# Spacing the indirect DMAs of an attention kernel with routed experts: scatters at eight places over four steps, and the tail's sends deferred over twelve buffers

## What is computed

```python
h = layernorm(x) * (1 + ca) + sa
x = x + ga * attention(h)       # 16 heads of 8, causal softmax, layernorm, output projection
h = layernorm(x) * (1 + cb) + sb
x = x + gb * experts(h)         # 8 experts; each token goes to the best 2 by bid
# experts: sum over the 2 chosen of w_e * (silu(h @ gate_e.T) * (h @ up_e.T)) @ down_e.T
```

## Time and profile before

| | |
|---|---|
| median of 3 runs | 632.87 us (631.29 to 634.27) |
| the profiled execution | 636.49 us; its span from first to last instruction 634.7 us |
| mean granted TensorE clock | 0.945 of full |
| busy share of the span | TensorE 89%, VectorE 74%, ScalarE 64%, GpSimd 38% |
| indirect DMAs | 64 scatters, 71 sends, about 1 us of GpSimd each |

### The profile page before, as it was taken

How to read it: one execution, slowest core, us unless ns; L and a number is a source line. 1 busy time by engine, 2 the same in 40 slices (tenths; PEclk the granted TensorE clock), 3 DMA queues, 4 the chain that set the end, 5 groups by cost and what they waited for, 6 DMA issues and landing times.

```text
span 634.7 us, 16553 instructions
## 1 busy us (share of the span) xinstructions
PE 565.4 (89%) x5257; PEld 424.8 (67%) x5258; DVE 471.2 (74%) x1592; ACT 405.9 (64%) x716; POOL 244.1 (38%) x328
## 2 busy tenths in 40 slices
PE   5778999999898998998998987999888999999940
PEld 3455565666465565564564546999887999999930
DVE  5898787899797787796896863687765666667636
ACT  4425787878777786786786775686534655655612
POOL 5401301133723615416326243456554333343326
PEclk9597999999999898998998996999989999999975
DMA  4442668432333232322323011111321211111138
GB/s 125 132 121 70 176 173 224 130 110 74 95 93 93 82 93 72 103 77 71 106 82 93 3 36 27 40 44 53 103 78 53 53 50 50 42 50 50 40 124 289
DMA packets 61511, 56.82 MB, mean 90 GB/s; under 512 B 11156, under 2 KB 55572, under 8 KB 61444
## 3 DMA queue, kind: packets, MB, share of 16 engines
q1 hardware_dynamic: 56548, 44.88, 25.5%
q0 software_dynamic: 4320, 8.99, 4.3%
q10 hardware_dynamic: 576, 2.10, 0.8%
HBM read 36.92 MB, written 18.45 MB: 87 GB/s over the span
## 4 chain that ended last, share of the span: by engine, by line
PE 75%; DVE 6%; DMA 5%; issue 4%; ACT 3%; another core or an unknown queue 2%; SPq 2%; POOL 1%; ACTq 0%; POOLq 0%; DVEq 0%
PE psN L962 18%; PE psO L565 11%; PE psO L973 9%; PE psT L546 7%; PE psN L531 6%; PE psT L548 5%; PE psN L533 4%; PE psM L573 2%; ACT probs L1090 2%; DMA probs<-expert_out 2%; PE psM L591 2%; DVE negm L1408 1%; PE psM L614 1%; PE psM L596 1%
## 5 line engine op out<-in xcount | busy, mean ns | idle before, releaser
L1408 DVE TENSOR_REDUCE negm<-psN 128x1 f32<-128x512 f32 (+3 forms) x352 | 211.4, 634 | 49.6 <-PE psN L533 48.7
L1090 ACT ACTIVATE probs<-psT 128x512 f32<-128x512 f32 x320 | 179.6, 595 | 56.0 <-PE psT L548 41.0
L962 PE MATMUL psN<-probs 128*128 128x128 f32 x1136 | 142.2, 279 | 3.0 <-ACT probs L1283 2.3
L962 PEld LDWEIGHTS psN<-probs 128*128 128x128 f32 x1136 | 135.8, 196 | 3.6 <-issue 3.5
L546 PE MATMUL psT<-qst_all,kst_all 74*128 74x256 bf16 (+2 forms) x384 | 100.9, 281 | 13.4 <-ACT probs L1090 12.0
L2146 POOL DMA_INDIRECT expert_out<-kst_all,dest x71 | 69.2, 975 | 112.2 <-DVE kst_all L1914 107.6
L531 PE MATMUL psN<-kst_all,qst_all 74*128 74x256 bf16 (+2 forms) x384 | 102.2, 283 | 6.8 <-DVE negm L1408 4.1
L565 PE MATMUL psO<-probs,vaug 128*32 128x512 f32 (+3 forms) x1024 | 97.0, 458 | 0.1
L533 PE MATMUL psN<-kst_all,qst_all 117*128 117x128 bf16 x512 | 92.9, 225 | 0.0
L1283 ACT ACTIVATE probs<-gu_w 128x1024 f32 x71 | 74.9, 1056 | 25.4 <-PE psN L962 21.5
L1890 DVE TENSOR_TENSOR probs<-probs,psN 128x512 f32<-128x512 f32 x71 | 48.7, 686 | 53.0 <-PE psN L962 27.9
(11 more groups left out here) (241 smaller groups left out, 743.2 us busy)
## 6 DMA issues: line engine op xcount, KB each, us to landing
qst_all<-q_parts_dram SPq DMA_DIRECT2D x96, 96.0 KB
kst_all<-k_parts_dram SPq DMA_DIRECT2D x96, 96.0 KB
kst_all<-dispatched SPq DMA_DIRECT2D x71, 66.0 KB
q_parts_dram<-qparts SPq DMA_DIRECT2D x24, 128.0 KB, 2.4
k_parts_dram<-kparts SPq DMA_DIRECT2D x24, 128.0 KB, 1.8
xall<-in_x SPq DMA_DIRECT2D x8, 256.0 KB, 3.4
gu_w<-in_gateT SPq DMA_DIRECT2D x4, 512.0 KB, 5.1
gu_w<-in_upT SPq DMA_DIRECT2D x4, 512.0 KB, 4.9
```

The lines of the kernel that those rows point to most:

```text
L962: mm = pe.matmul(bank[par][:, c * P:(c + 1) * P], ew[par][:, half, c * P:(c + 1) * P], xgT[par], start=True, stop=True)
L1090: nc.scalar.activation(probs[:, g % 2, 512 * u:512 * (u + 1)], psT[:, u % TBANKS, :], ACT.Exp, scale=SOFTMAX_SCALE).then_inc(exp_done, 1)
L1408: nc.vector.tensor_reduce(dst, src, axis=AX.X, op=ALU.max, negate=True).then_inc(nat_done, 1)
```

## The change

**Scatters.** `scatter_step` goes; `scatter_at` puts a batch's eight scatters at `SCATTERS`: three in step 3 of batch `b+2`, two in step 0, two in step 1 and one in step 2 of batch `b+3`. `rows` and `slots` become two of each, and the semaphore `dispatched` one for each of the two. The last five scatters of batch 5 fall into the tail's head (slots 1, 3, 5, 7, 9), those of batch 6 into slots 12 to 19, those of batch 7 into slots 19 to 25. `add_attn` now stands ahead of step 3's scatters.

**Sends.** `ysb` and `dest` become twelve (`Y`), used in turn up to tile 41. In slots 13, 15, ..., 25 GpSimd sends nothing; in slots 26, 28, ..., 38 it sends two tiles. For that, turns 5 and 6 are written out too (`HEAD_ALL` = 7).

**Into the tail.** SiLU's table is loaded ahead of the last attention values. VectorE, not ScalarE, copies the first tile's weights (`first_weights`), at the end of the last step. The rows of padding are filled at the start of that step, not in its middle. Some small tables move into the place of `xn`.

```diff
+SCATTERS = ((3, 0), (3, 4), (3, 8), (0, 3), (0, 9), (1, 2), (1, 9), (2, 4))
+IN_LAST = sum(g == G - 1 for g, _ in SCATTERS)
+IN_TAIL = (1, 3, 5, 7, 9)
+NEXT_TAIL = (12, 13, 14, 15, 16, 17, 18, 19)
+LAST_TAIL = (19, 20, 21, 21, 22, 23, 24, 25)
+NO_SEND = (13, 15, 17, 19, 21, 23, 25)
+TWO_SENDS = (26, 28, 30, 32, 34, 36, 38)
...
 def h_shift(b):
     hold("pool", pool, h2_chain, b + 1)
-    if has_earlier(b) and rows_of(b) is rows:
-        hold("pool", pool, dispatched, 16 * 2 * TB * b)
+    if 2 <= b < B - 1:
+        pool.wait_ge(dispatched[b % 2], 16 * 2 * TB * (b // 2))
...
-def scatter_step(b, g, c):
-    if g in (2, 3) and has_batch(b - 2):
-        pool.wait_ge(exp_done, UNITS * (4 * b + g) + probs_block(CHUNKS[c])[2])
-        scatter(b - 2, TB * (g - 2) + c)
+def scatter_at(b, g, unit):
+    i = SCATTERS.index((g, unit))
+    sent = b - 2 if g == 3 else b - 3
+    if has_batch(sent):
+        if unit:
+            pool.wait_ge(exp_done, UNITS * (4 * b + g) + unit)
+        scatter(sent, i)
...
 # GpSimd's tail, in ahead(j)
-    if 10 <= j < 10 + 2 * TB:
-        scatter(L - 1, j - 10)
-    if 18 <= j < 18 + 2 * TB:
-        scatter(L, j - 18)
+    for b, slots_taken, first in ((L - 2, IN_TAIL, IN_LAST), (L - 1, NEXT_TAIL, 0), (L, LAST_TAIL, 0)):
+        for i, slot in enumerate(slots_taken):
+            if slot == j:
+                scatter(b, first + i)
...
-for j in range(N1):
+tiles_sent = 0
+for j in range(N_ALL):
     ahead(j)
-    send(*divmod(j, U))
-with pool.Fori(HEAD, TURNS - 1) as i:
+    for _ in range(0 if j in NO_SEND else 2 if j in TWO_SENDS else 1):
+        send(*divmod(tiles_sent, U))
+        tiles_sent += 1
+with pool.Fori(HEAD_ALL, TURNS - 1) as i:
...
 # ScalarE, after all_steps
 h_norm(B - 2, (2, 3))
+nc.scalar.preload_act_table(ACT.Silu)
 keep_values(B - 1, 3)
...
-nc.scalar.preload_act_table(ACT.Silu)
 act.wait_ge(ew_in, 16 * 12)
 act.wait_ge(tiles_ready, 1)
 act.wait_ge(pv_done, TB * (STEPS - 1))
-keep_weights(0, 0)
...
 # VectorE, end of the last step
+def first_weights():
+    dve.wait_ge(ew_in, 16 * 12)
+    dve.wait_ge(pv_done, TB * (STEPS - 1))
+    e = dve.value_load(tile_w_i[0:1, 0:1], min_val=0, max_val=NX - 1)
+    V.tensor_copy(ew[0].rearrange("p k f -> p (k f)"),
+                  gu_w[:, bass.ds(e, 1)].rearrange("p o k f -> p (o k f)")).then_inc(ew_first, 1)
```

More of the change, by code:

```diff
@@ L182, in adaln_attention_moe @@
         pri = sb("pri", [P, NX])
-        rows = sb("rows", [P, TB, ROW])
+        rows = [sb(f"rows{i}", [P, TB, ROW]) for i in range(2)]
         xn2 = sb("xn2", [P, TB, E])
@@ L199, in adaln_attention_moe @@
         base = sb("base", [P, NX])
-        slots = sb("slots", [P, 2, TB], I32)
+        slots = [sb(f"slots{i}", [P, 2, TB], I32) for i in range(2)]
         slots_last = sb("slots_last", [P, 2, TB], I32)
@@ L221, in adaln_attention_moe @@
         dsc = [sb(f"dsc{i}", [P, 4]) for i in range(U)]
-        dest = [sb(f"dest{i}", [P, 1], I32) for i in range(U)]
+        dest = [sb(f"dest{i}", [P, 1], I32) for i in range(Y)]
         ew_in, fc_in = sem("ew_in"), sem("fc_in")
@@ L239, in adaln_attention_moe @@
         y_full, dsc_chain, y_ready = sem("y_full"), sem("dsc_chain"), sem("y_ready")
-        y_out = [sem(f"y_out{i}") for i in range(U)]
+        y_out = [sem(f"y_out{i}") for i in range(Y)]
         yp_in = [sem(f"yp_in{i}") for i in range(B)]
@@ L327, in slots_of, with dispatched_before @@
         def slots_of(b):
-            return slots_last if isinstance(b, int) and b == B - 1 else slots
+            return slots_last if b == B - 1 else slots[b % 2]
+        def dispatched_before(eng, b):
+            for i in range(2):
+                eng.wait_ge(dispatched[i], 16 * 2 * TB * len(range(i, b, 2)))
         passed = {e: sem(f"passed_{e}") for e in ("sp", "pe", "dve", "pool")}
@@ L359, in all_steps, with y_at @@
                 step(s // G, s % G)
+        def y_at(i, u):
+            if isinstance(i, int) and i < HEAD_ALL:
+                return (U * i + u) % Y, (U * i + u) // Y
+            return u, i + (len(range(u, N_ALL, Y)) - HEAD_ALL)
         def pairs_in(eng, first):
-            for u in range(U):
-                eng.wait_ge(y_out[u], 16 * (TURNS if u < LAST else TURNS - 1))
+            for u in range(Y):
+                sent = len(range(u, N_ALL, Y))
+                if u < U:
+                    sent += TURNS - HEAD_ALL - (u >= LAST)
+                eng.wait_ge(y_out[u], 16 * sent)
             for b in range(first, B, 2):
@@ L497, in _ @@
             sp.wait_ge(tiles_ready, 2)
-            sp.wait_ge(dispatched, 16 * 2 * NT)
-            with sp.Fori(HEAD, TURNS - 1) as i:
+            dispatched_before(sp, B)
+            for j in range(N1, N_ALL):
+                tile_in(*divmod(j, U))
+            with sp.Fori(HEAD_ALL, TURNS - 1) as i:
                 for u in range(U):
@@ L997, in _ @@
             pe.wait_ge(tiles_ready, 2)
-            with pe.Fori(HEAD, TURNS - 1) as i:
+            for i in range(HEAD, HEAD_ALL):
+                turn(i)
+            with pe.Fori(HEAD_ALL, TURNS - 1) as i:
                 turn(i)
@@ L1312, in _ @@
                 between(j)
-            with act.Fori(HEAD, TURNS - 1) as i:
+            for i in range(HEAD, HEAD_ALL):
+                turn(i)
+            with act.Fori(HEAD_ALL, TURNS - 1) as i:
                 turn(i)
@@ L1895, in weights @@
                 dve.wait_ge(xg_in[u], 16 * (i + 1))
-                if not (isinstance(i, int) and i == 0):
-                    dve.wait_ge(y_out[u], 16 * i)
+                r, sent = y_at(i, u)
+                if not (isinstance(i, int) and sent == 0):
+                    dve.wait_ge(y_out[r], 16 * sent)
                 m = xg[u]
@@ L1935, in _ @@
                 weights(*divmod(j, U))
-            with dve.Fori(HEAD, TURNS - 1) as i:
+            for i in range(HEAD, HEAD_ALL):
+                turn(i)
+            with dve.Fori(HEAD_ALL, TURNS - 1) as i:
                 turn(i)
```

106 lines of the change are left out of this document (61 added, 45 removed).

## The result

The changed kernel takes 616.95 us (median of 5 runs, 616.56 to 618.19). The ratio to the kernel before is 0.9748, 95% interval 0.9726 to 0.977. It is 15.9 us faster where 26.9 were forecast. The profiled execution took 616.82 us, its span is 615.1, so 19.6 less than the 634.7 of before.

What follows compares the result with a forecast made beforehand. TensorE, busiest at 89%, was taken to lose time to late completions while indirect DMAs follow closely. Terms -17.6 - 3.2 - 1.0 - 2.7 - 3.9 + 1.5 = -26.9 took span 634.7 to 607.8; forecast 606 us, range 599 to 620.

Steps and rivals of the forecast that it cites:

- the tail's head: First 27 tail tiles: a row of 21 DMAs replaces fours with pauses; net +1.5 us, bounds -6 and +10.
- main case: The forecast without rivals: 599 to 613 us, with the tail -6 to +5 and the start 0 to -3.9; chance 0.63.
- rival 1: The tail's long row costs as two or more fours would: +10 to +16, not +1.5; 614 to 621 us; chance 0.15.
- Steps 3 and 0 of attention: Attention, scatters at eight spaced places: steps 3 save 17.6 us, step 0 of batches 3 to 6 saves 3.2.
- at least 2.5 us apart: Sign that the prediction is right: the attention part's DMA_INDIRECTs stand at least this far apart.
- Rival 2: Attention's step 3 falls only to 12.3 us, not 10.6, losing 8.5 over five steps; 614 us; chance 0.12.
- rival 3: Indirect DMAs cost by number, not spacing, so attention keeps its 20.8 us loss; 627 to 629 us; chance 0.06.
- Two row buffers: Step 0 of batch 7: the shift's 5.10 us wait for batch 4's scatters goes; -1.0 us, bounds 0 and 5.1.
- step 3 of batch 7: Three spaced scatters of batch 5 remain where eight were issued; the chain's unknown wait goes, -2.7 us.
- into the tail: Between last attention values and first gate matmul: start 2.1 us earlier, plus 1.8 for the low clock; -3.9 us.
- Rival 4: Slower: each DMA in the tail's row of 21 holds TensorE's completions, from 1.7 us each; 633 to 645 us; chance 0.04.
- Two turns unrolled: Tail loop, two more turns written out: 0, or up to 0.5 us for a later fetch.

Runs made afterwards that it cites:

- run 3: The changed kernel with batch 1's scatters in four pairs, batch 2's in two fours, batch 3's as one row of eight; 634.54 us.
- run 8: The changed kernel plus eight extra DMAs in a row in step 3 of batches 3 (indirect, 4-byte rows), 4 (plain), 5 (indirect, 512-byte rows); 647.65 us.
- Run 6: The changed kernel with the padding rows filled in the middle of the last step again, as before the change; 615.21 us, ratio 0.9734.
- run 11: The changed kernel itself, timed again on a chip where the kernel before took 605.89 us; 600.56 us, ratio 0.989.
- run 4: The kernel of run 1 with sends of tiles 41 to 59 collected into rows of two, four and eight, singles between; 622.38 us.
- run 2: The changed kernel with no send put off: one send in every tail slot, none with two; 611.63 us, ratio 0.974.
- run 5: The changed kernel itself, timed again as base on a chip where the kernel before took 631.87 us; 616.36 us, ratio 0.975.
- run 1: The changed kernel with GpSimd waiting in each written-out tail slot until the tile before is weighed; 610.67 us, ratio 0.9719.
- run 9: The changed kernel with the waits of run 1, the filling of Run 6, and two-send slots three apart; 598.56 us, ratio 0.9871.

## Why the prediction was right or wrong

In the spans the change is -20.6 us up to batch 7, -7.5 to the gate matmul of tile 1, +6.6 in the tail's head, +0.3 to tile 70 and +1.6 behind it, in sum -19.6. The forecast had -20.8, -7.6, +1.5 and nothing for the last two. So the attention half held in its mechanism, and the miss is the tail's head first of all. That the time lies inside the range is owed to the range's width, not to the tail: +6.6 is over the main case's bound of +5 and under rival 1's +10, and 616.95 falls into rival 1's 614 to 621 only with 1.6 us at the kernel's end and 3.6 us of reference time that have nothing to do with it.

*Steps 3 and 0 of attention* (-17.6 and -3.2): right. Batch 7 begins 20.6 us earlier, 20.8 were forecast. Single scatters with 2.2 us or more between them cost nothing that a step shows (10.61 to 10.75). They are closer than the 2.7 to 5 us that I gave them, and in step 3 of batch 7 two even stand 1.28 us apart (352.23 and 353.51), so "at least 2.5 us apart" was not met, without harm. Rival 2 (steps 3 only at 12.3) fell with it. So did rival 3 (number, not spacing), most plainly in run 3. The Trainium skill's page "DMA: Bandwidth & Descriptors" (Latency and other measured facts) guesses that all DMA engines fetching GpSimd's descriptors make some SBUF ports busier; it says so to explain two slower DMA engines, not a late TensorE. Read as a cost by number, as I did, it has no support in run 8: plain DMAs from GpSimd's queue cost 1.0 us for eight, indirect ones 12 to 13 for a row of ten.

*Two row buffers, step 3 of batch 7, into the tail* (-1.0, -2.7, -3.9): right in sum, wrong inside. From the start of batch 7 to the gate matmul of tile 1 were 49.5 us (343.67 to 393.20) and are 42.0, -7.5 against -7.6. Step 0 of batch 7 gave 1.0 as forecast (10.33 to 9.35). Step 3 of batch 7, to the end of the last values, gave 3.8 instead of 2.7, the start 3.0 instead of 3.9: the first gate matmul came 1.4 us behind the last values (4.0 before), at full clock, but the next tile's gate matmul 4.2 us after it (4.6 before). The step that failed is "that memset moves a few places earlier, ahead of a normalise whose reader comes after all scores: nothing, or 1.8 if that is wrong". I looked for the reader of the normalise. The row statistics stand behind the filling too, and through GpSimd's shift they feed ScalarE, which has the table load, the last values and the weight copies in its queue behind them: 3.14 us idle at 360.45. Run 6 takes 2.4 us back. The bound of 1.8 was also a little short.

*The tail's head* (+1.5): this is the failed step that made the miss. "At the rate of today's fours ... 0.38 each ... 21 cost 8.0" took the price per DMA to be constant. With no loss from them the changed head takes 86.76 us (run 11), 8.3 less than the head before, so the share given to the DMAs before, about 7 us, seems well sized, if the two heads are alike otherwise. The changed head, at 101.68, holds 14.9 us of such loss where I had 8.0 and up to another 0.5. By runs 3, 4 and 8 the price of one DMA grows with the row: under 0.2 us in a pair, 0.2 in a three, 0.5 in the tail's five, 1.0 to 1.2 in attention's fours and eight, 1.3 in its ten. Why a four in the tail before looked cheap (0.38 each) is not shown; I take it that the pause behind it let TensorE catch up. That is rival 1's mechanism, forecast at +10 to +16 in place of +1.5; measured +6.6, of which run 2 leaves 3.6 without any deferral. And the row did not come as one of 21: it broke in three (8, 8 and 5), each time at a send that waited 2.2 to 2.9 us for its tile. Where nothing was lost (run 11) it came as one of 27. Rival 4 asked for 1.7 us a DMA; 1.3 was the most seen.

*Two turns unrolled* (0): right. Tiles 28 to 69 take 117.4 us, 117.1 before.

*Not in the sum:* from the gate matmul of tile 70 to the span's end are 30.9 us, 29.3 before. The chain holds the same links, the same 11.5 us transfer of the results among them, and its last GpSimd operation ends 1.5 us longer before the end of the span. What fills this time I didn't find out; it is there in the other traces of the changed kernel too (30.9 in run 5, 30.8 in runs 6 and 11).

*The reference time:* the profiled execution before was 3.6 us above its median, the one after at its median, so 19.6 us of span became 15.9 of time. I had taken this off the forecast.

*What the change is worth elsewhere:* where the kernel before takes 606 us the gain is 5.3 us, close to the 4.9 that I gave to what is not spacing (-1.0 and -3.9). I have no trace of the kernel before from there, so this split is argued, not shown. The other 10 to 11 us of the gain repair a loss that was there on three of five occasions (the first result, runs 1 to 4, runs 5 to 8). If close indirect DMAs are all that differs, they cost 26 us before (632 against 606) and 16 after (617 against 601).

*Best version:* run 9's kernel, 3.3 us below the changed one where both ran (597.21 against 600.56, with no overlap of their runs). Where close DMAs cost it wasn't run; run 1, with a part of its edits, took 610.67 there.

## What to carry to other kernels

Price a row of back-to-back indirect DMAs by how long it is, not by a constant per member. Where the effect showed at all, pairs and threes (up to 3.8 us) cost 0 to about 1 us, and from four on TensorE stood idle for the row's length less 3 to 5 us, with a low clock behind it that cost 0.7 to 4 more. Taking waits away from a queue (a send that is put off no longer waits) makes such rows longer, so look at what then stands back to back, and leave a wait in. When an operation is moved ahead of another, follow everything that stands behind it on the engine, not only the next reader. And time the kernel before beside every run: two occasions can differ by 4% on the very thing that is tuned.

## What the runs showed of the hardware that was not expected

- A row of indirect DMAs from GpSimd (1.27 us each) makes TensorE's completions late, by 5.3 us in a row of ten. Late in a row, gate matmuls in the tail also come singly, 1.4 us apart in one row and 0.7 in another, instead of 0.12. Loss by row: 0 to 0.35 us for a pair, 0.6 to 1.1 for a three, 2.4 for five in the tail, 3.9 and 5.0 for four in attention, 9.3 for eight, 9.6 for nine in the tail, 12.0 and 13.3 for ten. Singles 2.2 us apart cost nothing.
- The size of the rows hardly matters (4 bytes: 12.0 us, 512 bytes: 13.3, for ten), and eight plain GpSimd DMAs in 4.34 us cost at most 1.0; a longer row of plain ones wasn't run.
- The effect was there on three occasions and absent on two, once with the same chip number. The same kernel took 616.36 and 600.56 us, and a row of 27 in 34 us cost next to nothing in the second case. What differs between them the traces don't tell.
- The low clock follows the holds: 0.88 in a step with a row of four, 0.74 with eight, 0.70 with ten, and 1.00 in the same steps and in the whole head where nothing was held.
